# Attention products in float32 on four 32-row strips of TensorE, in place of one bfloat16 product with 72 split rows

## The reference

```python
def attn(x, ...):                      # per layer; b=1, t=2048, 16 heads, head_dim 8
    q, k, v = heads(x @ Wq), heads(k_of(x)), heads(v_of(x))   # layer 0: rope, latent k and v; layer 1: per-head 8x8 weights
    scores = einsum('bhqd,bhkd->bhqk', q, k) / sqrt(8)
    scores = where(causal, scores, -inf)
    attn = softmax(scores, axis=-1)
    return einsum('bhqk,bhkd->bhqd', attn, v) ... @ W_o
```

## Time and profile before

| what | us |
|---|---|
| median of 3 runs | 1527.86 |
| fastest of them | 1524.72 |
| span of the profiled execution | 1517.5 |
| attention of the first layer in it (first max product to last output product) | 493.25 |
| attention of the second layer | 490.10 |

### The profile page before, as it was taken

One profiled execution on the slowest core, in us unless ns is written; L12 is line 12 of the kernel. 1 busy time (PEld: TensorE's weight loads), 2 busy tenths in 40 slices (PEclk: granted clock), 3 DMA queues, 4 the chain that ended last, 5 costly groups with the idle time before them and its releaser, 6 DMA issues. The chain is left out here.

```text
span 1517.5 us, 20983 instructions
## 1 busy us (share of the span) xinstructions
PE 1211.4 (80%) x7346; PEld 524.4 (35%) x7347; DVE 951.7 (63%) x2598; ACT 683.7 (45%) x895; POOL 187.9 (12%) x257
## 2 busy tenths in 40 slices
PE   2917999999799998319553899999989999676984
PEld 2502333333233343207421223233333334444663
DVE  6627888888678772301163788888868775342443
ACT  1302465665566666103230445566656667421331
POOL 4110000000000000344410000000000000054442
PEclk9857999999899999559875899999999999777997
DMA  4154000230502000022216310140120000011113
GB/s 128 31 118 68 16 16 15 39 74 16 67 15 73 3 3 1 22 63 57 76 50 123 52 43 19 35 87 25 26 44 2 3 3 2 1 35 43 47 47 104
DMA packets 41740, 64.10 MB, mean 42 GB/s; under 512 B 5440, under 2 KB 27872, under 8 KB 41328
## 3 DMA queue, kind: packets, MB, share of 16 engines
q1 hardware_dynamic: 37328, 53.95, 16.4%
q0 software_dynamic: 4320, 8.92, 1.7%
HBM read 45.55 MB, written 18.92 MB: 42 GB/s over the span
## 5 line engine op out<-in xcount | busy, mean ns | idle before, releaser
L792 ACT ACTIVATE probs_at<-st 128x1024 f32<-128x1024 f32 (+3 forms) x640 | 545.7, 897 | 382.4 <-PE st L747 236.4
L810 DVE TENSOR_REDUCE mxp_at<-mx 128x1 f32<-128x512 f32 x768 | 498.4, 685 | 96.0 <-PE mx L716 95.1
L716 PE MATMUL mx<-ks,qs 128*128 128x512 bf16 (+3 forms) x1280 | 379.9, 368 | 84.9 <-DVEq L801 33.2
L747 PE MATMUL st<-qs,ks 128*128 128x512 bf16 (+3 forms) x1280 | 355.6, 354 | 13.9 <-DMA qs<-shrow_at 12.6
L812 DVE CUSTOM_DVE_ANT_0 junk_at<-mx,maskN 128x384 f32<-128x384 f32 (+3 forms) x512 | 241.2, 485 | 104.7 <-PE mx L716 102.4
L763 PE MATMUL av<-probs_at,vs 128*32 128x512 f32 (+3 forms) x2560 | 301.7, 543 | 0.2
L716 PEld LDWEIGHTS mx<-ks,qs 128*128 128x128 bf16 x1280 | 104.8, 98 | 437.7 <-DVE mxp_at L810 183.6
L747 PEld LDWEIGHTS st<-qs,ks 128*128 128x128 bf16 x1280 | 123.4, 99 | 111.0 <-ACT probs_at L792 21.8
L1027 POOL DMA_INDIRECT perm<-rows,pos x64 | 63.3, 989 | 512.6 <-SPq L1136 248.4
L750 PE MATMUL st<-maskTb,identb 128*128 128x128 bf16 x512 | 100.9, 222 | 0.0
L763 PEld LDWEIGHTS av<-probs_at,vs 128*32 128x32 f32 x2560 | 50.6, 108 | 107.2 <-issue 96.7
(11 more groups left out here) (232 smaller groups left out, 1027.8 us busy)
## 6 DMA issues: line engine op xcount, KB each, us to landing
qs<-q_parts SPq DMA_DIRECT2D x63, 128.0 KB
ks<-k_parts SPq DMA_DIRECT2D x18, 384.0 KB
w_sb<-in_w_dram SPq DMA_DIRECT2D x16, 256.0 KB, 3.1
q_parts<-part_pj SPq DMA_DIRECT2D x12, 256.0 KB, 3.0
k_parts<-part_pj SPq DMA_DIRECT2D x12, 256.0 KB, 4.7
perm<-in_pad_dram SPq DMA_DIRECT2D x1, 2600.0 KB, 11.6
rows_f<-perm SPq DMA_DIRECT2D x39, 65.0 KB, 1.8
ks<-k_parts SPq DMA_DIRECT2D x12, 192.0 KB
```

Source lines behind the costliest of these rows:

```text
L716: pe.matmul(buf[:, 0:w], QS[p][:, j, (4 * Q + qb) * P:(4 * Q + qb + 1) * P], KS[p][:, j, c * CH:c * CH + w], start=True, stop=True).then_i ...
L747: mm = pe.matmul(st[half][:, y, off:CH], KS[p][:, j, kb * P:(kb + 1) * P], QS[p][:, j, Q * CH + off:(Q + 1) * CH], start=True, stop=True, ...
L792: act.activation(probs[:, s % 2, 2 * half:2 * half + 2, off:CH], st[half][:, :, off:CH], ACT.Exp, scale=SCALE).then_inc(exp_done[half], 1)
L810: ins = v.tensor_reduce(dst, buf[:, 0:w], AX.X, ALU.max)
```

## The change

q and k stay float32. Each has one resident copy for all groups, `QT` and `KT`, of 128 partitions by 4 groups by 2048. Head j of a group has partitions 32j to 32j+7; partition 32j+8 holds the shift in `QT` and ones in `KT`. Products of head j run on the 32-row strip j of TensorE with 8 rows (maxima) or 9 rows (scores), 128 columns wide. The projection stores q and k per chunk of 512 columns and reads them back with four DMAs each. The split into three parts, its work on ScalarE, VectorE and POOL, and the reloads of groups go. The turn is a float32 transpose whose copy is now ScalarE's, as is the copy of `attT`. `probs` has three buffers, `mxp`, `mx` and the shift row have two (before four). `UNITS` is in another order, the maxima go around the heads innermost, and the planner is another one: it keeps a time for each strip and gives orders for TensorE and ScalarE. On the diagonal both masks of a half follow both of its score products.

Cut to its core ("..." where lines are left out):

```diff
-UNITS = [(0, 0), (0, 1), (0, 2), (1, 1), (0, 3), (1, 2), (1, 3), (1, 0),
-         (2, 2), (2, 3), (3, 3), (2, 1), (3, 1), (2, 0), (3, 0), (3, 2)]
+UNITS = [(g, Q) for Q in (1, 0, 2, 3) for g in range(NG - 1)] + [(NG - 1, Q) for Q in (3, 2, 1, 0)]
...
-    return [(g, Q, j, qb, c) for qb in range(TPC) for j in range(GH) for c in range(Q + 1)]
+    return [(g, Q, j, qb, c) for qb in range(TPC) for c in range(Q + 1) for j in range(GH)]
...
+        if what == "max":
+            u, x = maxes[k]
+            w = max_width(x)
+            pe = max(t, pe) + .03
+            rows[x[2]] = pe + w / 1200
+            dve = max(dve, rows[x[2]] + lat) + .08 + w * .00104
...
+        elif what == "scores":
+            off = step_off(s)
+            pe = max(t + .1, pe) + .06
+            rows[2 * half] = rows[2 * half + 1] = done = pe + (CH - off) / 1200
+            if on_diagonal(s):
+                pe = done = max(rows) + .2
+                rows = [done] * GH
...
+        elif what == "values":
+            pe = max(t, pe)
+            rows = [pe + (CH - step_off(a)) / 1200 + .05] * GH
...
+                g.memset(m.KT[:], 1.).then_inc(pool_set, 1)
+                g.memset(m.VS[:], 0.).then_inc(pool_set, 1)
...
+                def store(n):
+                    i, c = steps[n]
+                    sp.wait_ge(flat_ready[i], s4 + c + 1)
+                    sp.dma_start(dram[f"{'qk'[i]}{L}"][:, cols(c)], qf[i][:, cols(c)]).then_inc(stored[n % 2], 16)
+
+                def load(n):
+                    i, c = steps[n]
+                    sp.wait_ge(stored[n % 2], 16 * (s4 + n // 2 + 1))
+                    for j in range(GH):
+                        sp.dma_start((m.QT, m.KT)[i][RT * j:RT * j + HD, :, cols(c)], bass.AP(
+                            dram[f"{'qk'[i]}{L}"].tensor, j * HD * T + c * CH, [[T, HD], [GH * HD * T, NG], [1, CH]])).then_inc(m.sem(f"heads_in{c}"), 16)
...
-                        pe.matmul(buf[:, 0:w], QS[p][:, j, (4 * Q + qb) * P:(4 * Q + qb + 1) * P],
-                                  KS[p][:, j, c * CH:c * CH + w], start=True, stop=True).then_inc(mx_ready, 1)
+                        pe.matmul(buf[:, 0:w], QT[row(j, HD), g, (4 * Q + qb) * P:(4 * Q + qb + 1) * P], KT[row(j, HD), g, c * CH:c * CH + w],
+                                  start=True, stop=True, tile_position=(RT * j, 0)).then_inc(mx_ready, 1)
...
-                        mm = pe.matmul(st[half][:, y, off:CH], KS[p][:, j, kb * P:(kb + 1) * P], QS[p][:, j, Q * CH + off:(Q + 1) * CH],
-                                       start=True, stop=True, skip_group_check=diag)
-                        if diag:
+                        mm = pe.matmul(st[half][:, y, off:CH], KT[row(j, HD + 1), g, kb * P:(kb + 1) * P],
+                                       QT[row(j, HD + 1), g, Q * CH + off:(Q + 1) * CH], start=True, stop=True, tile_position=(RT * j, 0),
+                                       skip_group_check=on_diagonal(s))
+                    if on_diagonal(s):
+                        for y in range(2):
                             mm = pe.matmul(st[half][:, y, off:off + P], m.identb[:], m.maskTb[:], start=False, stop=True, skip_group_check=True)
...
+                def turned(k):
+                    kind, x = ROT[k]
+                    buf, free = mxb[k % MXBUF], mx_free[k % MXBUF]
+                    act.wait_ge(mx_ready, RB + k + 1)
+                    if kind == "attT":
+                        act.copy(attT[:], buf[:]).then_inc(free, 1)
...
+                        act.copy(shrow[:, n % 2], buf[0:GH, :]).then_inc(shift_row, 1)
```

More of the change, by code:

```diff
@@ L73, in step_off, with on_diagonal @@
     return max(0, STEPS[s][2] * P - STEPS[s][1] * CH)
+def on_diagonal(s):
+    return STEPS[s][2] >= TPC * STEPS[s][1]
 def schedule():
[L79 to L95, removed]
+    maxes = [(u, m) for u, (g, Q) in enumerate(UNITS) for m in max_tiles(g, Q)]
+    last_max = [max(k for k, (x, _) in enumerate(maxes) if x == u) for u in range(NU)]
+    lat = .15
+    pe = dve = act = 0.
+    rows = [0.] * GH
+    free = [0.] * MXBUF
+    exp_done, probs_ready = [0., 0.], [None] * NST
+    ready, evacuated = [None] * NU, [None] * NU
@@ L96, in schedule @@
+    av_free = 0.
     normed = [0] * NC4
-    while k < len(base) or s < NST or norms:
+    chores = []
+    pe_order, act_order, rot = [], [], []
+    k = s = half = a = 0
+    while k < len(maxes) or s < NST or a < NST or chores:
         b = len(rot) % MXBUF
[L99 to L102, removed]
-            free[b] = dve
-            out.append(("rot", len(rot)))
-            rot.append((kind, x))
[L106 to L157, removed]
@@ L158, in schedule @@
-    return out, rot, pe
-ORDER, ROT, _ = schedule()
+        all_rows = max(rows)
+        found = []
+        if chores:
+            t, kind, x = min(chores)
+            found.append((max(pe, t, all_rows, free[b] + lat) - .2, "chore"))
+        if s < NST and ready[UNIT[s]] is not None and s < a + PB:
+            found.append((max(pe, ready[UNIT[s]] if STEPS[s][2] == 0 else 0., exp_done[half] + lat, rows[2 * half], rows[2 * half + 1]) - .1, "scores"))
+        if a < NST and probs_ready[a] is not None:
+            found.append((max(pe, probs_ready[a] + lat, all_rows, av_free + lat if STEPS[a][2] == 0 else 0.), "values"))
@@ L333, in project @@
         hT = sb("hT", [P, T])
-        qf, res = [sb(f"qf{i}", [P, CH]) for i in range(2)], [sb(f"res{i}", [P, CH]) for i in range(2)]
-        parts = [[sb(f"part{i}{a}", [P, T], BF) for a in range(3)] for i in range(2)]
+        qf = [sb(f"qf{i}", [P, T]) for i in range(2)]
         xn = sb("xn", [P, TILES, D])
@@ L393, in _ @@
+                store(0)
+                for n in range(1, NS):
+                    store(n)
+                    load(n - 1)
+                load(NS - 1)
             @block.tensor
@@ L553, in _ @@
                     for n in range(NS):
-                        step(n)
-                    residue(NS - 1)
+                        rope(n)
                 else:
@@ L1517, in layout @@
     ang = (np.arange(T, dtype=np.float32)[None, :] * inv[:, None]).astype(np.float32)
-    ones = np.zeros((GH, 2 * GH, T), np.dtype("bfloat16"))
-    for j in range(GH):
-        ones[j, 2 * j:2 * j + 2] = 1
     dw = np.zeros((E8 + 1, 3 * P, D), np.float32)
@@ L1527, in layout @@
         "x": a["L0_attn_x"][0], "cos": np.cos(ang).astype(np.float32), "sin": np.sin(ang).astype(np.float32),
[L1528 removed]
+        "pad": pad,
         "mod": np.concatenate([a["L0_c"].T, a["L1_c"].T, a["L0_wmod"], a["L1_wmod"]], 1),
```

424 lines of the change are left out of this document (177 added, 247 removed).

## The result

The changed kernel takes 2817.46 us (median of 4 runs, 2814.97 to 2820.72); the kernel before took 1526.82 beside it (median of 4, one of them the 4729.34 us named above). The ratio is 1.8446 [1.8411, 1.8482]. Far slower, as the direction said, but 950 us beyond the forecast and outside the range of 1500 to 2060.

What follows compares the result with a forecast made beforehand. TensorE and VectorE were taken to share the bound, coupled by three PSUM buffers. Span 1517.5 + 389 (attention at 686 us a layer) - 45 (earlier starts) = 1861 us; forecast time 1865, range 1500 to 2060.

Steps and rivals of the forecast that it cites:

- A product occupies its strip for 0.85 us: Attention stages: a float32 product of 512 columns takes four times a bfloat16 one; four strips work side by side.
- The walk of six intervals: Four-column-block unit, between values products: six intervals with 13 score halves and 23 maxima take 23.9 us.
- Steps off the diagonal at 3.67: Attention, per layer: 96 steps of two score halves, maxima beside them included, at 3.67 us each: 352 us.
- Steps on the diagonal at 219/64 = 3.42: Attention, per layer: 64 steps, masks draining the strips after each half: 53 x 3.6 + 11 x 2.6 = 219 us.
- Maxima in trains at 0.62: Attention, per layer: 170 maxima in runs of nine or more, nothing beside them, paced by buffer rounds: 105 us.
- What stands ahead of the first values product and behind the last: Attention, per layer: turns, the output products and the ends together take 10 us.
- The lower bound of a layer: Attention stage priced at the lower ends of its steps and maxima: 551 us a layer, 1600 us in all.
- What goes away: Before the attention stages: first maximum near 82, 28 us earlier; second layer 17 us less; 45 us saved.
- The order: New planner: charges a strip 0.43 us for 512 columns, where the trace shows 0.85, and values 0.48 against 1.00.
- Rival 1: Row strips: record pairs start in order, 0.43 us per product; 720 us a layer, about 1940 in all; chance 0.12.
- Rival 2: Row strips stay full, waiting products let later ones pass; 468 us a layer, 1435 in all, faster; chance 0.14.
- Rival 3: Row strips don't run side by side at all: 1144 us a layer, near 2790 in all; chance 0.06.

Runs made afterwards that it cites:

- the run with full rows: Changed kernel with products addressing 31 rows (maxima) and 32 (scores) of each strip instead of 8 and 9, added rows zero in QT: 1933.67 us, ratio 1.2796.
- The kernel with one drain: Changed kernel with 31 and 32 rows, corrected planner costs, and all four scores of a diagonal step before its four masks: 1826.83 us, ratio 1.2055.
- the first six experiments: Full rows, 1933.67 us; kernel before on 8 rows, 2258.41; then corrected planner costs, 1890.44, plus joined diagonal halves, 1826.83, or no masks, 1767.15; those costs at 8 rows, 2724.19.
- the last two: Changed kernel with 31 and 32 rows, added rows zero in both operands: 1955.75 us; kernel before with part of q loaded after the second projection piece: 1511.15 us.

## Why the prediction was wrong, point by point

**The step that failed** is the assumption, made in the paragraph on what bounds the kernel and carried into every price, that the granted clock in the stages stays at 0.95. It is named among the signs that would prove the forecast wrong, and it fell to 0.51. In the same order at full rows a stage takes 715.9 and 714.9 us (forecast 686); at 8 and 9 rows 1158.5 and 1159.9. Put into the sum, that difference is 2 x 444 = 888 us of the 952 missed. The forecast took its price of a product from one with 32 rows and read it at full clock, and did not ask what keeps the clock up. The earlier trace rows had a hint: the products there are at half clock for part of the projection (1.91 us), though that stretch has idle time as well and so does not tell rows from idleness.

**What the sizes were.** Here the run with full rows is the measure, as its order is the forecast's.
- A product occupies its strip for 0.85 us, and four do so side by side: right. Four score products in 0.96 us from start to start of the next group (487.25 to 488.21), three maxima likewise.
- The walk of six intervals, 23.9 us: measured 22.1 (4.86, 5.42, 2.92, 2.06, 2.05, 4.81 for 5.2, 5.35, 2.9, 2.0, 2.65, 5.75). At half clock the same six took 39.5.
- Steps off the diagonal at 3.67: in the first stage, 60 intervals between values products hold their scores with nothing but maxima beside them, 129 halves in 208 us, 3.23 for two halves. With the intervals that have turns in them, trains apart, 96 steps take about 316 us where 352 were forecast: 36 too much.
- Steps on the diagonal at 219/64 = 3.42: the 53 intervals with masks and without a turn have a mean of 3.88. All intervals that belong to the diagonal come to about 259 us: 40 too little. Masks and their drains were right in size (0.41 for a half, 0.45 measured). A maximum of 384 or 512 columns behind them takes 1.06 us and finds no cover.
- Maxima in trains at 0.62: too little at half clock. The stage has seven trains of nine or more, 146 maxima in 122 us with the turns among them, 0.83 each, where 170 were priced at 105: 17 too little. At full clock the price holds (from 534.13 on VectorE takes five in 3.19 us). The three longest trains, 100 maxima, have a clock of 0.50, 0.56 and 0.65 and take 0.86 to 0.91 for each; in one of them 20 products in 18.13 us, at a granted clock of 0.50:

```profile
98.81 18.13 PE L620 MATMUL mx<-kt,qt 31*128 31x256 f32 x40 [0.28 <-DVE mxp_at L733]
```

The price left out is again the clock. The kernel with one drain shows a train apart from the rest; ahead of it, in it and behind it, by stretch:

```profile
224.00:246.00 22.00, 21.76 (x185) 8.86 (x184) 12.51 (x34) 9.45 (x17) 0.00 (x0) 1.00 0.07 25
247.30:265.20 17.90, 17.90 (x49) 9.33 (x45) 13.89 (x30) 0.00 (x0) 0.00 (x0) 0.63 0.00 0
265.20:285.00 19.80, 19.13 (x70) 8.91 (x68) 10.34 (x26) 5.18 (x7) 0.00 (x0) 0.50 0.09 27
```

With maxima alone, up to three strips at a time, the granted clock falls from 1.00 (0.63 is the mean of the stretch), though TensorE has no idle time, and it is still 0.50 in the 20 us behind the train, where scores and values stand again. What stands ahead of the first values product and behind the last, trains apart, took 19 us where 10 were forecast. -36 + 40 + 17 + 9 are the 30 us by which the full-row stage exceeds 686: the sum comes near because its errors cancel, not because each price was right. The lower bound of a layer was also added up wrongly: its own prices give 541 us, not 551, and 1580 in all, not 1600. Nothing hangs on it.

**What goes away.** First maximum at 80.37 (forecast 82, before 109.85). In the second layer the way from the last output product to the first maximum is 195.1 us (1238.89 to 1433.96) instead of 212.8: 17.7 less (forecast 17).

```profile
80.37 2.08 PE L615 MATMUL mx<-kt,qt 8*128 8x512 f32 x6 [12.98 <-PEq L374]
...
1433.96 2.08 PE L615 MATMUL mx<-kt,qt 8*128 8x512 f32 x6 [10.49 <-PEq L374]
```

By these two 29.5 + 17.7 = 47 us are saved (45 were forecast); outside the stages the span has 35.6 less, so some 12 are given back. They lie behind the last output product: 223.1 us there, 211.5 before. In the first six experiments that stretch is 209 to 210.3, and it is 224.5 in the last two, of which one is the kernel before with its q loaded earlier. So the change need not be what makes it, and why some traces have it stays open. SP's loads are now issued in stride with the stores:

```profile
73.89 0.34 SPq L385 DMA_DIRECT2D k_heads<-qf_pj  x1
75.23 4.40 SPq L391 DMA_DIRECT2D kt<-k_heads  x8
```

**The order.** "The order is made for strips that come free twice as early" is true of the planner's figures, but little hangs on it: 43 us of 1934 when they are mended. The other order of the diagonal steps was worth more, some 64 us on top; whether a wholly different order would gain more was not tried.

**The rivals.** Rival 1 (products start 0.43 apart, 1940) is refuted by the same rows: four would need five times 0.43 = 2.1 us at full clock, and take 1.14, tail included. The rule of the Trainium skill that was quoted for it (TensorE: Matmul & The Clock Gate, "The mechanism") is that matmuls start and end in the order of the program, and the prediction read the trace of the column strips as contradicting it. That reading goes too far. In the full-row kernel the first records of the four products start at 487.245 to 487.265 and the second ones at 487.778 to 487.798: products in different strips overlap, but the records do not name their strip, so the trace neither confirms nor refutes that they keep their order. That the full-row kernel takes 1934 us is chance. Rival 2 (strips stay full, 468 us a layer) does not come about even with full rows, a mended order and no masks: 635. Rival 3 (no side-by-side work, near 2790) gave nearly the measured time by a mechanism that isn't there: the strips do overlap, and the clock is halved. A time that fits is no proof of a mechanism; one pair of rows of the timeline, 2.09 us for four products, tells them apart.

**What stays open.** The 142 and 151 us that remain in the stages without masks. It is argued, not shown, that long products with three PSUM buffers (a result comes 1.07 us after its start) and the clock in the trains make them. The clock can be a part only, by an estimate from the rows: 0.90 over 635 us means a fifth of them at the lower level, worth at most 63 us; the 0.95 over 493 us of the kernel before is worth 25 by the same sum, so it explains at most some 40 of the 142. A fourth buffer was not tried, nor how many rows between 9 and 31 are enough.

## What to carry to other kernels

Before a product on few rows takes the place of one on many, ask what it does to the clock of everything on TensorE; here 8 of 128 rows, or 8 of 32 in each strip, meant half clock at 99% busy, and products that nobody had touched took 1.94 us instead of 1.07. If the rows can be filled with zeros, address them: one memset and slices of 31 and 32 rows took the changed kernel from a ratio of 1.84 to 1.28. And look for the gain that a large change brings on the side: the earlier start could be had alone, and is the only part of the change that took time off the kernel before (ratio 0.987, a small gain).

## What the runs showed of the hardware

- The granted clock follows the rows that products address, in the cases tried. In stages where TensorE is 97 to 99% busy it was 0.51 with 8 or 9 rows (float32 in strips, two orders; bfloat16 without strips) and 0.89 to 0.92 with 31 or 32 rows in each strip. The contents of the rows made little difference: 0.91 and 0.89 in the two stages with zeros on both sides, 0.91 and 0.92 with ones in `KT`.
- With 31 rows but only maxima at work, up to three strips, it fell from 1.00 in a stretch of 17.9 us without idle time (mean 0.63), and was 0.50 in the 19.8 us behind it. How rows and strips combine was not measured.
- Float32 products in different row strips overlap almost fully, each with its two records: four in 1.14 us where one alone takes 1.02.
- Changing from strips to the whole array and back costs little: a diagonal half with two masks is 1.28 us, of which 0.85 are its strip and 0.11 the masks' columns, so 0.16 for each change.
